# Expert tiles of a two-layer network: sums gathered from the output and written back, in place of an accumulating scatter into a DRAM buffer

## What is computed

```python
logits = jnp.einsum('btd,de->bte', x, gate_w)
probs = jax.nn.softmax(logits, axis=-1)
expert_weights, expert_indices = jax.lax.top_k(probs, TOP_K)
expert_weights = expert_weights / expert_weights.sum(-1, keepdims=True)
for i in range(E):
    wi = jnp.where(expert_indices == i, expert_weights, 0.0).sum(-1)
    h = jax.nn.silu(jnp.einsum('btd,df->btf', x, w1[i])) * jnp.einsum('btd,df->btf', x, w3[i])
    out = out + jnp.einsum('btf,fd->btd', h, w2[i]) * wi[..., None]
...
x = x + _L1_ffn_ref(_layernorm(x, axis=-1), L1_ffn_gate_w, L1_ffn_w1, L1_ffn_w3, L1_ffn_w2)
```

## Time and profile before

| | us |
|---|---|
| median of 3 runs | 757.08 |
| lowest and highest | 752.0 and 757.09 |
| the profiled execution, its time | 756.54 |
| its span in the trace | 754.8 |
| expert tiles, from the first y to the last | 401.2 to 742.1 |
| copy to the output, issued | 746.34 |

### The profile page before, as it was taken

The page is one execution under the profiler, slowest core; times in us unless marked ns, Lnnn a source line. Parts: engine busy times, 40 slices in busy tenths (PEclk is TensorE's granted clock), DMA queues, the critical chain, the costliest instruction groups (busy, mean ns, idle before and its releaser), DMA issues.

```text
span 754.8 us, 17035 instructions
## 1 busy us (share of the span) xinstructions
PE 657.7 (87%) x4890; PEld 464.8 (62%) x4890; DVE 500.0 (66%) x1180; ACT 375.3 (50%) x878; POOL 291.9 (39%) x358
## 2 busy tenths in 40 slices
PE   2799999997777776898099999999999999999992
PEld 2588888886534545786056666666666666666661
DVE  6389899998588967797954746555464747554430
ACT  1366666665686643786223535363543635543320
POOL 3111111121153625577233736464553637543321
PEclk9799999999999999699589999999999999999996
DMA  8200000000300005336405253533415264421114
GB/s 282 47 15 14 14 14 14 14 0 1 112 0 1 0 1 172 128 82 226 135 23 174 49 150 76 150 85 84 140 31 153 73 181 126 116 43 29 31 15 125
DMA packets 47414, 59.01 MB, mean 78 GB/s; under 512 B 13328, under 2 KB 41168, under 8 KB 47056
## 3 DMA queue, kind: packets, MB, share of 16 engines
q1 hardware_dynamic: 39808, 47.72, 19.5%
q0 software_dynamic: 7536, 10.44, 7.8%
HBM read 145.96 MB, written 11.73 MB: 209 GB/s over the span
## 4 chain that ended last, share of the span: by engine, by line
PE 58%; DVE 20%; issue 8%; ACT 5%; DMA 2%; POOL 2%; DVEq 2%; ACTq 1%; SPq 0%; POOLq 0%
PE psum L1052 19%; PE psum L1074 11%; PE psum L752 5%; PE psum L1065 4%; PE psum L736 3%; PE psum L759 3%; PE psum L772 2%; ACT region L1346 2%; PE psum L791 1%; PE psum L741 1%; PE psum L714 1%; DVE region L1759 1%; DVE region L1777 1%; PE psum L779 1%; DVE region L1956 1%
## 5 line engine op out<-in xcount | busy, mean ns | idle before, releaser
L1052 PE MATMUL psum<-region 128*128 (+1 forms) x936 | 214.8, 379 | 1.6 <-DVE region L1952 1.6
L1052 PEld LDWEIGHTS psum<-region 128*128 128x128 bf16 x936 | 91.5, 98 | 95.5 <-DVE region L1952 1.2
L1329 ACT ACTIVATE region<-psum 128x512 f32<-128x512 f32 x78 | 46.5, 597 | 179.6 <-PE psum L1052 178.7
L675 POOL DMA_INDIRECT sum_dram<-region,row_token x39 | 75.2, 1927 | 135.3 <-DVE region L1948 135.3
L1074 PE MATMUL psum<-region 128*128 (+1 forms) x936 | 110.5, 275 | 5.3 <-DVE region L1956 5.3
L1074 PEld LDWEIGHTS psum<-region 128*128 128x128 bf16 x936 | 91.4, 99 | 18.9 <-issue 7.5
L1931 DVE TENSOR_TENSOR region<-psum,region 128x512 f32<-128x512 f32 x78 | 53.8, 690 | 68.3 <-ACT region L1329 68.3
L545 POOL TENSOR_TENSOR region<-region,pair_mask 128x256 f32<-128x256 f32 x32 | 21.3, 687 | 128.3 <-ACT region L1114 128.3
L1956 DVE TENSOR_TENSOR region<-psum,region 128x1024 bf16<-128x1024 f32 x39 | 47.6, 1221 | 17.7 <-ACT region L1337 17.5
L667 POOL DMA_INDIRECT region<-xrow_dram,row_token x39 | 41.4, 1062 | 38.0 <-DVE row_token L1917 13.6
L1421 DVE TENSOR_REDUCE region<-psum 128x8 f32<-128x1024 f32 x32 | 39.0, 1218 | 18.4 <-PE psum L752 18.4
(11 more groups left out here) (298 smaller groups left out, 1220.3 us busy)
## 6 DMA issues: line engine op xcount, KB each, us to landing
region<-in_L_ffn_w SPq DMA_DIRECT2D x117, 1024.0 KB
region<-in_ctx SPq DMA_DIRECT2D x32, 128.0 KB, 2.4
xrow_dram<-region SPq DMA_DIRECT2D x1, 2080.0 KB, 7.8
x_sb<-in_x SPq DMA_DIRECT2D x4, 512.0 KB, 8.0
region<-in_ctx SPq DMA_DIRECT2D x2, 1024.0 KB, 7.0
region<-neg_max_dram SPq DMA_DIRECT2D x1, 2048.0 KB, 11.5
sum_dram<-x_sb SPq DMA_DIRECT2D x1, 2048.0 KB, 7.5
region<-neg_max_dram SPq DMA_DIRECT2D x4, 256.0 KB, 4.0
```

Source lines behind the costliest of these rows:

```text
L675: pool.indirect_dma_start(sum_dram, bass.IndirectOffsetOnAxis(ap=row_token[:, t:t + 1], axis=0), y_d[:, t % 2, :], None, compute_op=ALU.ad ...
L1052: last = mm(psum[:, 2 * f + n, :], (xT_lo if xl else xT_hi)[:, p, k, :], weights_at(place, wl, n, k * F1 + f * FH, FH), start=(i == 0), st ...
L1329: act_fn(sil_d[:, f, :], psum[:, 2 * f, :], ACT.Silu).then_inc(sil_d_ready, 1)
```

## The change

The buffer `sum_dram` and its copy at the end are gone. `x_sb` is stored straight to the output. For each tile, GpSimd gathers the tile's rows from the output into a new SBUF tile `sums_sb`, VectorE makes y(t) as the weighted product plus these sums in one instruction, and a plain indirect DMA writes the result to the same rows. Since two tiles may hold the same token, the gather of tile t+1 waits until the write of tile t has landed; it also waits for y(t), because there is a single `sums_sb`. Rows that pad a tile are left out of both transfers by a bound check on the row number. Lines of the changed kernel stand some 1 to 14 higher.

```diff
+        sums_sb = sb("sums_sb", [P, D])
...
-        sum_dram = nc.dram_tensor("sum_dram", (B * P + P, D), F32, kind="Internal").ap()
...
+        out_rows = out.rearrange("b p d -> (b p) d")
...
-            sp.dma_start(sum_dram[B * P:B * P + P, :], empty_row[:, 0:D]).then_inc(rows_stored, 16)
...
-            sp.dma_start(sum_dram[0:B * P, :].rearrange("(b p) d -> p b d", p=P), x_sb[:]).then_inc(rows_stored, 16)
+            sp.dma_start(out_rows.rearrange("(b p) d -> p b d", p=P), x_sb[:]).then_inc(out_stored, 16)
...
             sp.wait_ge(sum_added, 16 * NT)
-            sp.dma_start(out.rearrange("b p d -> (b p) d"), sum_dram[0:B * P, :]).then_inc(out_stored, 16)
-            sp.wait_ge(out_stored, 16)
...
+            nc.gpsimd.memset(sums_sb[:], 0.0).then_inc(route_consts, 1)
...
-            def add_rows(t):
+            def gather_sums(t):
+
+                pool.wait_ge(sum_added, 16 * t)
+                if t >= 1:
+                    pool.wait_ge(y_ready, t)
+                pool.indirect_dma_start(sums_sb[:], None, out_rows, bass.IndirectOffsetOnAxis(ap=row_token[:, t:t + 1], axis=0),
+                                        bounds_check=B * P - 1, oob_is_err=False).then_inc(sums_loaded, 16)
+
+            def write_rows(t):
 
                 pool.wait_ge(y_ready, t + 1)
-                if t >= 1:
-                    pool.wait_ge(sum_added, 16 * t)
-                pool.indirect_dma_start(sum_dram, bass.IndirectOffsetOnAxis(ap=row_token[:, t:t + 1], axis=0),
-                                        y_d[:, t % 2, :], None, compute_op=ALU.add).then_inc(sum_added, 16)
+                pool.indirect_dma_start(out_rows, bass.IndirectOffsetOnAxis(ap=row_token[:, t:t + 1], axis=0),
+                                        y_d[:, t % 2, :], None, bounds_check=B * P - 1, oob_is_err=False).then_inc(sum_added, 16)
 
             pool.wait_ge(info_ready, 2)
-            pool.wait_ge(rows_stored, 64)
+            pool.wait_ge(rows_stored, 32)
...
             pool.wait_ge(info_ready, 1)
+            pool.wait_ge(out_stored, 16)
+            gather_sums(0)
             for t in range(NT - 2):
                 gather_rows(t + 2)
                 weights_low(t + 2, t % 2)
                 if t >= 1:
-                    add_rows(t - 1)
+                    write_rows(t - 1)
+                    gather_sums(t)
             for t in range(NT - 3, NT):
-                add_rows(t)
+                write_rows(t)
+                if t + 1 < NT:
+                    gather_sums(t + 1)
...
                 if t >= 2:
 
                     dve.wait_ge(sum_added, 16 * (t - 1))
-                nc.vector.tensor_scalar(y_d[:, p, :], psum[:, 7, 0:D], w_col[:, bass.ds(t, 1)], None, ALU.mult).then_inc(y_ready, 1)
+                dve.wait_ge(sums_loaded, 16 * (t + 1))
+                nc.vector.scalar_tensor_tensor(out=y_d[:, p, :], in0=psum[:, 7, 0:D], scalar=w_col[:, bass.ds(t, 1)],
+                                               in1=sums_sb[:], op0=ALU.mult, op1=ALU.add).then_inc(y_ready, 1)
```

More of the change, by code:

```diff
@@ L374, in build @@
         sum_added = sem("sum_added")
+        sums_loaded = sem("sums_loaded")
+        out_rows = out.rearrange("b p d -> (b p) d")
         block = stack.enter_context(nc.Block())
@@ L465, in _ @@
             sp.wait_ge(x3_ready, B)
-            sp.dma_start(sum_dram[0:B * P, :].rearrange("(b p) d -> p b d", p=P), x_sb[:]).then_inc(rows_stored, 16)
+            sp.dma_start(out_rows.rearrange("(b p) d -> p b d", p=P), x_sb[:]).then_inc(out_stored, 16)
             sp.wait_ge(xrow_routed, 3)
-            sp.wait_ge(route_consts, 16)
+            sp.wait_ge(route_consts, 17)
             sp.dma_start(xrow_dram[0:B * P, :].rearrange("(b p) c -> p b c", p=P), xrow).then_inc(rows_stored, 16)
@@ L646, in _ @@
             nc.gpsimd.iota(xrow[:, :, D:D + 1].bitcast(I32), pattern=[[P, B], [0, 1]], base=0, channel_multiplier=1).then_inc(route_consts, 1)
-            pool.wait_ge(route_consts, 16)
+            pool.wait_ge(route_consts, 17)
             pool.indirect_dma_start(xg[:, 1, 0:D], None, x.rearrange("b p d -> (b p) d"),
@@ L1024, in _ @@
             pe.wait_ge(chosen_ready, 1)
-            pe.wait_ge(route_consts, 16)
+            pe.wait_ge(route_consts, 17)
             chosen_v = chosen_b[:].rearrange("p b e -> p (b e)")
@@ L1819, in _ @@
             over_b = lambda v: v.unsqueeze(1).to_broadcast([P, B, E])
-            dve.wait_ge(route_consts, 16)
+            dve.wait_ge(route_consts, 17)
             nc.vector.tensor_copy(iota_e, int_tmp[:, 0:E])
```

## The result

| | before | after |
|---|---|---|
| median of 4 runs, us | 756.99 | 776.12 |
| lowest and highest | 752.0 and 757.09 | 771.01 and 779.93 |
| the profiled execution, its time | 756.54 | 771.01 |
| first y to last y | 340.9 | 365.1 |
| last y to the end of the span | 12.7 | 4.5 |

The ratio is 1.026 (95% interval 1.022 to 1.030): slower. The end of the kernel gained 8.2 us and the stage of the expert tiles lost 24.3, which is 3.5 for each of the seven reloads in the mean (2.6 to 3.9 in the first five, by the starts of the down matmuls). The part ahead of the stage, which the change hardly touches, was 1.5 shorter in the profiled execution. Over all its executions, one in a much slower state at 1363 us left out, the kernel before took 752 to 762, with a mean granted clock of 0.96 in the shortest and 0.94 in the longest.

A forecast was written before the change was run, and what follows sets the result against it. TensorE, fed by VectorE, was taken to pace the kernel. Profiled 756.5 minus 8.0 (copy) minus 0.5 (last write) plus 20.3 (seven reloads at 2.9) gave 768.3; the median's 0.5 made it 769, range 748 to 786.

The forecast's parts named there:

- the sum: Whole kernel: profiled 756.5, minus 8.0 for the copy, minus 0.5 for the last write, plus 7 x 2.9 = 20.3: 768.3.
- the turn: Expert stage: cycle from y through write and gather to the next y, 7.05 us undisturbed, hidden in a plain tile's 8.89.
- Rival 3: Expert stage: write-and-gather cycle paces every tile, 30 us more plus some 5 per reload; about 810, chance 0.08.
- the signs: Trace marks: sums awaited only in each reload's second tile, TensorE idle some 3 us there, L694 2.7 later against y.
- The end: Kernel's end: 8.0 us less without the copy, 0.5 less because the last write lands in 3.0 instead of 3.5.
- W: Plain write from issue to landing: 3.0 us, between a plain store's 2.2 and the accumulating add's 3.8.
- The two handovers: In the cycle: 0.75 us from y's start to the write's start, 0.3 for GpSimd to go on after landing.
- The write under the fetch: Reload: write of tile 15 meets a weight fetch and lands in 6.0 us (bounds 3.0 and 6.3).
- the second rival: Reload: write of tile 15 lands in 4.5 us, 1.5 lost per reload; 759, chance 0.14.
- The two steps one behind the other: Reload: GpSimd's 3.81 and VectorE's 2.29 us subtractions run in sequence, 6.1 whichever is first; next write 2.6 late.
- The size: Reload: y(17) 4.0 us late, less 1.06 to spare, so that tile's down matmuls come 2.9 late, seven times.
- Rival 1: Reload: write escapes the fetch, write plus gather landing (W + G) within 5.6 us, nothing lost; 748, chance 0.16.

The follow-up runs named there:

- e8: Changed kernel with GpSimd's gather of sums and write put behind its gather of x rows and weights step; 794.31 us, ratio 1.050.
- e5: Changed kernel with the low half of weight part 0 made by VectorE instead of GpSimd; 774.48 us, ratio 1.023.
- e1: Kernel before with the accumulating add going straight to the output, with bound check, and no copy at the end; 753.1 us, ratio 0.996.
- e7: Kernel before with bound-checked adds straight to the output, no copy, and only the last tile gathered, summed and plainly written; 752.51 us, ratio 0.994.
- e2: Changed kernel with sums gathered from x a tile ahead into two buffers, no gather waiting for a write, running sum left out; 747.74 us, ratio 0.989.
- e3: Changed kernel without bound check on gather of sums and write, rows in a buffer with spare rows, end copy back; 762.85 us, ratio 1.008.
- e10: Changed kernel with weight fetches cut to an eighth, no bound check, spare-row buffer and end copy back; 754.05 us, ratio 0.998.

## Why the prediction was right, and what in it was wrong

The forecast was 769 (748 to 786) and slower with 0.68; measured 776. Against the profiled execution, which the sum was made for, it was 768.3 against 771.0. That execution was the fastest of the four, 5 below their median, with a mean granted clock of 0.956; the other three have 0.950, 0.943 and 0.949. So they ran more at the lower clock, but where is in no trace. It can be in the stage, as in e8 and in part in e5. It can as well be ahead of it: the profiled execution of e1, the longest of its nine, has its first y at 406.1 with a clock of 0.90 up to 399 us, that of e7 at 399.7 with 0.93, and both have the same stage of 340.5.

**Which mechanism.** Right: the turn of write and gather fits into a plain tile and not into a reload. Plain tiles kept 8.89, and without the turn nothing is lost (e2). Rival 3, the turn pacing every tile, did not come, though the bound check that it named was real. Two of the signs did not come either. The waits were to stand in the second tile of each reload only; y waited 17 times, and most of TensorE's idle time was one tile earlier. And L694 was to start 2.7 later against y; it started 7.04 after y(15), where it was 6.83. Against TensorE it was 2.3 late, because y(15) was.

**Luck in the size.** The sum gave 20.3 us to the fetch alone, with nothing for the check. With the fetch as it is and no check (e3) the stage lost 10.2. The sum had the fetch at twice its cost and left the check at nothing, and the two came out near the measured 24.3.

**The end.** Right: minus 8.5 was predicted, 8.2 measured. That too was partly luck: I did not see that the drain would have eaten 5 of these had the adds stayed.

**The turn.** 7.05 was predicted for an undisturbed one, 7.89 measured. W, the write, was taken as 3.0 and is 2.4 to 2.5 (2.2 for the tiles of padding at the end, which move next to nothing); it is the lower bound, the plain store, that it stands near. The two handovers, 0.75 and 0.3, are 1.33 and 0.8: the bound check. The gather and the waking of VectorE, 3.0 together, are 3.28. I had named the check as absent from the trace and put it under rival 3 alone, where it should have been in the sum with bounds of its own. It was the larger part of the loss.

**The write under the fetch.** The step that failed: "A plain write issued at the same moment meets the same fetch, so W = 6.0 here". The write of tile 15 landed in 2.4, because it was out before the fetch began:

```profile
DMA to landing us min/median/max: 2.4/2.4/2.4
```

It was the write one tile earlier that met a fetch, of an earlier part. Issue to landing of the write of 537.04, and the queues between 537.2 and 540.8 (packets, MB, share; no other queue):

```profile
DMA to landing us min/median/max: 5.9/5.9/5.9
```

```profile
q1 hardware_dynamic: 369, 1.45, 101.3%
```

Again the software queue moved nothing for more than 3 us, as in the earlier trace rows. The Trainium skill (DMA: Bandwidth & Descriptors, "Queues, rings and completion order") has the engines take their queues in turn; the trace does not bear that out here either, and the second rival, which put the landing midway, is not what happened. The lateness reached GpSimd's weights step all the same, now by a plain tile that used all of its 2.1 spare. The size of the meeting was right, its place was one tile off, and L701, which is L694 of the kernel before, is again ready just as VectorE starts its own step.

**The two steps one behind the other.** Right in mechanism: 3.81 + 2.29 in a row. But I counted the cost on the write of tile 16 only ("2.6 us late"), and let the order of the two be indifferent. It is not: GpSimd came first, so VectorE's step ended at 559.75, and y(16) and the low half of h, which stand behind it, held TensorE for 2.67 in tile 16 already. The Trainium skill (SBUF — State Buffer, "SBUF: two separate sides") says that a GpSimd operation that reads SBUF and a VectorE operation with two SBUF inputs each hold a port pair for the whole instruction, the later one blocked; the 5.58 us of L1923 agree.

**The size.** Predicted 2.9 a reload in its second tile; measured 3.5, of which 2.3 in the tile ahead and 1.2 in that one. Over seven that is 24.3 where the sum had 20.3.

**The Trainium skill's figure for a transfer.** The estimate of 2.3 us worked out from the Trainium skill (DMA: Bandwidth & Descriptors, "Anatomy of one DMA — SWDGE (gpsimd) path") is close to the write's 2.4, against what the prediction says of it. The gather of sums, from its start to y, takes 3.28. Rival 1 needed W + G = 5.6 and had 2.4 + 3.2, at its very edge; the 1.1 of the check put the turn beyond it. With check and fetch both gone (e10) its case came: nothing is lost.

## What to carry to other kernels

Replacing an accumulating transfer by a read, an add and a write turns a queue of independent operations into a loop of landings; add up that loop with every handover in it, and compare it with the shortest interval that it must fit, not with the mean one. Whatever waits for a landing inside such a loop delays everything behind it on its engine's queue, and other transfers that start then will meet new neighbours. Before a copy at the end is removed, look for what it covers.

## What the runs showed of the hardware beyond that

- A bound check on an indirect transfer from GpSimd costs 0.55 us where the transfer stands behind a wait (1.33 against 0.75 from y to the write, 3.28 against 2.72 from the write to the gather), none that shows where it stands right behind another issue (0.30 in e2), and next to nothing in the issue itself (1.01 to 1.02 with, 0.97 to 1.01 without).
- GpSimd's drain at the end takes 8.3 us behind accumulating indirect adds (7.8 where the last transfer is a plain write) and 2.8 to 3.1 where all are plain.
- A plain indirect write of 128 KB lands in 2.4 to 2.5 us, the accumulating one in 3.8; both take some 6 under a weight fetch of the sync queue (5.4 and 5.9, and 6.3 in the earlier trace rows).
- A gather's issue on GpSimd goes from 1.0 to 1.8 under a VectorE step with two inputs in SBUF (e5), a write's from 1.0 to 2.3 in the changed kernel (at 568.89) and to 2.8 in e10.
